# One pair of tiles in 97 fetched row by row from the sync queue, with a ring of 16 slots and frees that lag eight pairs

## The chip, the cores and the metric

The kernel runs on one core of a Trainium2 chip. The metric is the device time of one execution in microseconds (us), as the median of several; "ns" is nanoseconds. The engines are TensorE (PE; its weight loads are shown as PEld), VectorE (DVE), ScalarE (ACT), GpSimd (POOL) and SyncE (SP). Each has its own instruction queue with its own sequencer, which also executes the register arithmetic and the branches of that engine's loops. In rows of the trace a "q" behind the engine (PEldq, SPq) marks such an instruction.

## The reference, cut to what matters

It is one layer of a graph network with 6250 nodes of 256 values and 100,000 edges `src, dst`, ordered by `dst`:

```python
xn = layernorm(x)
h = norm * (xn @ W.T + bias)              # norm = rsqrt(1 + degree of the node)
agg = segment_sum(h[dst], src)            # 100,000 gathered rows, summed by src
x = x + norm * (agg + h) + linear_attention(xn) * gate @ Wproj + bproj
x = x + ffn(layernorm(x))                 # for the nodes with the best scores alone
```

The feed-forward part is computed for every node and added only to the nodes with the highest scores (KEEP = 6250 / 2 - 1 of them). The part that matters here is `h[dst]` summed by `src`: 100,000 rows of a table in HBM have to be fetched and added into 6250 sums.

## The kernel before

The work falls into four stages. First (to about 235 us) normalisation, degree histogram and gate, while VectorE sorts the edges by the window of their `src` node (a window is 125 nodes, there are 50). Then (to about 340 us) TensorE and ScalarE compute `h` and store it as `table` in HBM, 6250 rows of 512 float16 values (the high and the low part of 256 values), 1 KB each; this overlaps with attention sums until about 381 us. The third stage is the long one, to about 1339 us. The last is the selection and the store of the output.

In the long stage the 100,000 edges stand in 782 tiles of 128, taken in pairs: 391 pairs ("blocks" in the code, `NBLK`). Four queues work on them in step:

- **GpSimd** (lines 425 to 435) issues one indirect DMA for each tile: 128 row numbers from a column of `col_of`, 128 rows of `table` into one slot of `gath`. Ahead of a pair it waits for the semaphore `freed`.
- **SyncE** (lines 374 to 383) waits for the landing of each pair in order and adds 1 to `arrived`. Then, for the first 34 pairs at each and later at every fourth, it loads from `due_row` how many visits TensorE must have made to be done with the pair `LAG` = 3 back, waits for `visits` to reach that, and raises `freed`. The ring is `ROUND` = 17 pairs of slots.
- **VectorE** builds, for each visit, two 128x128 one-hot matrices (line 1271) in a ring of `HOTS` = 8 visits.
- **TensorE** adds the pair into the window's sums in bank 0 with two 128x512 matmuls (line 812). A pair that lies on the border of two windows is visited in both: 458 visits. The loop is a real one (`counted`, lines 303 to 313): each turn has a few instructions of the sequencer. Line 309 holds five register operations in one fused instruction (the copy of the counter, the counter plus 1, `made`, `q % ROUND`, `made % HOTS`), line 812 twice a fused instruction of six multiplications and additions that make the two addresses, and line 312 the branch.

Around the visits of window `w` TensorE does the feed-forward of the window before and the attention and projection of the next (`window`, lines 872 to 885), and the projection needs what VectorE makes from the sums just finished (`summed`, `normed`, `gated`). Before its visits each window loads three numbers (lines 796 to 798) and adds its own rows (line 802).

Of the kernel before, what the change touches and what calls it, by code (L numbers as in the profile page):

```python
# [10 lines left out]
I32 = mybir.dt.int32  # L11
# [4 lines left out]
NODES, C, EDGES = 6250, 256, 100000  # L16
# [16 lines left out]
NB = 34  # L33
GROUP = 2
GEDGE = GROUP * TILE
ROUND = NB // GROUP
HOTS = 8
NOH = HOTS * GROUP
NBLK = (EDGES + GEDGE - 1) // GEDGE
NROUND = NBLK // ROUND  # L40
assert NROUND * ROUND == NBLK
PAD_ROW = NODES + 3 * NW - 1
LAG = 3
NXR = 4
DUE_MAX = 32000
LEVELS_IN_GROUP = 5
# [19 lines left out]
SEARCH = sum(STEPS)  # L66
FREED_BY = 4
FREED_ALONE = 2 * ROUND
NB_KT = 2
PEEK_FROM, PEEK, PEEK_LEAD = 10, 12, -26  # L70
PEEK_DEALT, KMAX_AFTER = 10, 16
# [19 lines left out]
def gps_layer(nc, x, src, dst, W, bias, Wqkv, Wproj, bproj, ln_g, ln_b, Wg1, bg1, Wg2, bg2,  # L91
              wr, br, w1, b1, w2, b2, out):
    table = nc.dram_tensor("table", (NODES, PART), F16, kind="Internal").ap()
    ctx = ExitStack()
    with ctx:
        def sb(name, shape, dt=F32):
            return ctx.enter_context(nc.sbuf_tensor(name, shape, dt))

        def sem(name):
            return ctx.enter_context(nc.semaphore(name))  # L100
# [13 lines left out]
        col_of = sb("col_of", [128, COLS], I32)  # L114
        row_of = sb("row_of", [128, COLS])
        e_int = keyB[0:EP, 0:EC].bitcast(I32)
        gath = sb("gath", [128, NB, PART], F16)
# [81 lines left out]
        gate_tmp = sb("gate_tmp", [128, NBLK])  # L199
        hg = gate_tmp[0:P, 2 * P:2 * P + 2 * GH].rearrange("p (j n) -> p j n", j=2)  # L200
        due_row = gate_tmp[0:1, :].bitcast(I32)
        table_of = sb("table_of", [P, 1])
        hgT = gate_tmp[0:GH + 1, 0:2 * P].rearrange("p (j n) -> p j n", j=2)
        kmax = sb("kmax", [128, 2])
# [13 lines left out]
        def part_of(n):  # L218
# [10 lines left out]
        xb = W_in[0:P, 0, :]  # L229
# [28 lines left out]
        names = ("edges wload wdown wmain const const2 wtp wev hotr hist stats normd rowsh wss wsc diag nwt bn bna bg1 kps cntp chain "  # L258
                 "counted tabs final issued outs xn tp hid main hgv gtp ghT gps gate hev split xstore "
                 "moved kT kmaxd cntd kmt kmx kmr kv ekv xnr ctxp sumcp sumtp sumtc vdone ctxn wqcp wqcd pads ranked dealt oh arrived visits freed due duerow selfused "  # L260
                 "op og pp xb xm sum xh low x1 st nt zed ge zwt ztp zT hp gelu yp yv base halves csum").split()
        s = {n: sem("s_" + n) for n in names}
        s_block = [sem(f"s_block{k}") for k in range(ROUND)]
        s_xr = [sem(f"s_xr{j}") for j in range(NXR)]
        s_hself = [sem(f"s_hself{j}") for j in range(2)]
        s_xt = [sem(f"s_xt{j}") for j in range(2)]
# [48 lines left out]
        @block.sync  # L315
        def _(sp):
            halves = ((0, SPRAY), (SPRAY, P))
            for lo, hi in ((0, SPRAY), (SPRAY, EP)):
                sp.dma_start(e_int[lo:hi, 0:EW], src_v[lo:hi, :]).then_inc(s["edges"], 16)
            for lo, hi in ((0, SPRAY), (SPRAY, EP)):  # L320
                sp.dma_start(col_of[lo:hi, 0:EW], dst_v[lo:hi, :]).then_inc(s["edges"], 16)
            sp.wait_ge(s["pads"], 2)
            for to, of in ((e_int, src_s), (col_of, dst_s)):
                sp.dma_start(to[0:EP:EP // (GROUPS * SPARE), EW:EW + 1], of).then_inc(s["edges"], 16)
            for q in range(NXL):
                for lo, hi in halves:
                    sp.dma_start(big_g[lo:hi, q * XCH:(q + 1) * XCH, :],
                                 x_v[lo:hi, q * XCH:(q + 1) * XCH, :]).then_inc(s_x[q], 16)
            late = [
                (proj[:, :, :], Wproj.rearrange("(c p) n -> p c n", p=128)),  # L330
                (bproj_bc[:, :], bproj.rearrange("(a n) -> a n", a=1).to_broadcast([P, C])),
                (b2_bc[:, :], b2.rearrange("(a n) -> a n", a=1).to_broadcast([P, C])),
                (wr_bc[:, :], wr.rearrange("n a -> a n").to_broadcast([P, C])),
                (br_bc[:, :], br.rearrange("(a n) -> a n", a=1).to_broadcast([P, 1])),
            ]
            for to, of in late:
                sp.dma_start(to, of).then_inc(s["wload"], 16)
            with nc.allow_non_contiguous_dma(reason="a short vector onto partitions"):
                sp.dma_start(b1_sb[:, :], b1.rearrange("(c p) -> p c", p=128)).then_inc(s["wload"], 16)

            sp.wait_ge(s["hist"], NHIST + 1)
            sp.wait_ge(s["xstore"], HELD)
            for n in range(HELD // 8):
                sp.dma_start(big_t[:, n * 8:(n + 1) * 8, 0:2 * P],
                             held[n][:, 0:8 * 2 * P].rearrange("p (w c) -> p w c", w=8)).then_inc(s["moved"], 16)
            sp.wait_ge(s["moved"], 16 * (HELD // 8))
            sp.wait_ge(s["kT"], HELD // 2)
            sp.dma_start(w1_sb[:, :, :], w1.rearrange("(c p) n -> p c n", p=128)).then_inc(s["wload"], 16)

            sp.wait_ge(s["ranked"], 1)  # L350
            for c, lo, hi in hands:
                to = (lo + c * LANES) % EP
                sp.dma_start(dealt_keys[to:to + hi - lo, c * HAND:(c + 1) * HAND],
                             ranked_keys[lo:hi, c * HAND:(c + 1) * HAND]).then_inc(s["dealt"], 16)

            def table_rows(m):
                n = m % NPARTS
                sp.wait_ge(s["split"], m + 1)
                for lo, hi in row_parts:
                    sp.dma_start(tab_v[lo:hi, m, :], part_of(n)[lo:hi, :, :].rearrange("p a c -> p (a c)")).then_inc(s_tab[n], 16)  # L360

            for m in range(NW):
                table_rows(m)

            sp.wait_ge(s["tabs"], 1)
            sp.sem_inc(s["freed"], ROUND)

            sp.wait_ge(s["due"], 1)
            sp.wait_ge(s["gate"], NW)
            sp.dma_start(due_row[0:1, :].rearrange("a (i k) -> a i k", k=ROUND), visits_due[0:NROUND, :]).then_inc(s["duerow"], 16)  # L370
            sp.wait_ge(s["xnr"], NW)
            sp.dma_start(w2_sb[:, :, :], w2.rearrange("(c p) n -> p c n", p=128)).then_inc(s["wdown"], 16)
            sp.wait_ge(s["duerow"], 16)
            freed = ROUND
            for q in range(NBLK):
                sp.wait_ge(s_block[q % ROUND], 16 * GROUP * (q // ROUND + 1))
                sp.sem_inc(s["arrived"], 1)  # L377
                free = ROUND + q + 1 - LAG
                if freed < free and freed < NBLK and (q < FREED_ALONE or q % FREED_BY == 0):
                    due = sp.value_load(due_row[0:1, q:q + 1], min_val=1, max_val=DUE_MAX)  # L380
                    sp.wait_ge(s["visits"], due)
                    sp.sem_inc(s["freed"], free - freed)
                    freed = free
            for lo, hi in out_groups:
                sp.wait_ge(s["final"], hi)
                sp.dma_start(out_v[0:SPRAY, lo:hi, :], big_g[0:SPRAY, lo:hi, :]).then_inc(s["outs"], 16)
            sp.wait_ge(s["outs"], 2 * 16 * len(out_groups))

        @block.gpsimd
        def _(g):  # L390
# [31 lines left out]
            for n in range(NPARTS):  # L422
                g.wait_ge(s_tab[n], tab_landed(NW, n))
            g.wait_ge(s["tabs"], 1)
            for q in range(NBLK):
                if q * GROUP == FIRST_LANES * LANES:
                    g.wait_ge(s["tabs"], 2)
                if q == ROUND - 6 // GROUP:
                    g.wait_ge(s["vdone"], 1)
                g.wait_ge(s["freed"], q + 1)  # L430
                for tile in range(q * GROUP, (q + 1) * GROUP):
                    g.indirect_dma_start(  # L432
                        out=gath[:, tile % NB, :], out_offset=None, in_=table[:, :],
                        in_offset=bass.IndirectOffsetOnAxis(ap=col_of[:, tile:tile + 1],
                                                            axis=0)).then_inc(s_block[q % ROUND], 16)

        @block.scalar
        def _(a):
# [190 lines left out]
        def _(t):  # L629
# [164 lines left out]
            def sums(w, j, nth):  # L794
# [9 lines left out]

                with counted(t, f"sums{next(loops)}", first, end) as (q, upto):
                    made = q + before
                    for value in (made, q % ROUND, made % HOTS):
                        t.compute_val(value)
                    t.wait_ge(s["arrived"], upto)
                    slots, hot_slots = bass.ds(q % ROUND, 1), bass.ds(made % HOTS, 1)  # L810
                    for u in range(GROUP):
                        last = t.matmul(bank[0][:, 0:PART],  # L812
                                        onehot_g[:, hot_slots, u * 128:(u + 1) * 128].rearrange("p a r -> p (a r)"),
                                        gath_g[:, slots, u * PART:(u + 1) * PART].rearrange("p a c -> p (a c)"),
                                        start=False, stop=False, skip_group_check=True)
                        if u == 0:
                            last.wait_op(s["oh"], t.lower_val(made), "sem-ge")
                    last.then_inc(s["visits"], 1)
# [676 lines left out]
```

## Time and profile before

| what | value |
|---|---|
| median of 3 runs | 1404.43 us (1404.09 to 1404.56) |
| the profiled execution | 1399.99 us, span 1398.3 us |
| PE / DVE / POOL / ACT busy | 80% / 71% / 57% / 27% |
| mean granted TensorE clock | 0.931 |
| gathers on GpSimd | 782, busy 753.5 us, idle ahead of them 267.6 us |

Busy shares are means over stages that are bound by different things, so the long stage has to be read by itself. Idle time of an engine costs nothing unless something waits for that engine at that moment. Register, branch and semaphore instructions aren't counted as busy, so a loop that is paced by its sequencer shows as an engine with small gaps released by "issue".

### The profile page before, as it was taken

What the parts mean: (1) busy time and instruction counts of PE and PEld (TensorE: products, weight loads), DVE (VectorE), ACT (ScalarE), POOL (GpSimd) and SP (SyncE); (2) the same over time, 40 slices, a digit from 0 to 9 for tenths busy, and PEclk for the clock granted to TensorE, in tenths of its full rate; (3) what the DMA queues carried; (4) which work ended last, traced back from release to release, by engine and by line L of the source; (5) the groups of instructions that cost most, each with busy time, mean ns of one, the idle gap of its engine ahead of it and who ended that gap; (6) DMA issues with size and microseconds to landing.
All of it is one profiled execution on the core that took longest, in us unless ns stands there. A gap on an engine that the chain in (4) does not pass through costs nothing.

```text
span 1398.3 us, 27721 instructions
## 1 busy us (share of the span) xinstructions
PE 1115.0 (80%) x6477; PEld 812.5 (58%) x6478; DVE 994.5 (71%) x3592; ACT 373.3 (27%) x1168; POOL 802.9 (57%) x851
## 2 busy tenths in 40 slices
PE   0488998999977888888888888878887888778853
PEld 0488887888644555555555566546555555445532
DVE  8999999999546666666666665666665666566667
ACT  5844466665411111111111111111111111111100
POOL 0000002542777777777777777777777777777710
PEclk9789999999979999999999999999999999999976
DMA  9000211333633444333443443444434443444305
GB/s 240 20 2 2 90 43 45 108 100 92 184 113 112 117 120 120 114 115 118 119 119 117 119 119 110 119 117 119 118 111 119 120 119 112 117 117 119 112 27 183
DMA packets 76391, 149.81 MB, mean 107 GB/s; under 512 B 17984, under 2 KB 48416, under 8 KB 75708
## 3 DMA queue, kind: packets, MB, share of 16 engines
q0 software_dynamic: 37536, 102.55, 25.4%
q1 hardware_dynamic: 17190, 25.56, 6.3%
q10 hardware_dynamic: 21606, 21.05, 5.1%
q8 instruction: 21, 0.34, 0.1%
q14 instruction: 38, 0.30, 0.1%
HBM read 132.83 MB, written 12.80 MB: 104 GB/s over the span
## 4 chain that ended last, share of the span: by engine, by line
PE 28%; POOL 23%; issue 14%; DVE 11%; DMA 3%; DVEq 2%; ACT 1%; SPq 0%; POOLq 0%; ACTq 0%
POOL gath L432 23%; PE bank L812 9%; PE bank L868 3%; PE bank L857 3%; PE bank L742 3%; PE bank L750 3%; PE bank L734 3%; DMA gath<-table,col_of 3%; DVE onehot L1271 3%; DVE big_g L1470 1%; DVE rs L1325 1%; PE bank L835 1%; PE bank L827 1%; DVE rs L1327 1%; DVEq L1271 1%
## 5 line engine op out<-in xcount | busy, mean ns | idle before, releaser
L432 POOL DMA_INDIRECT gath<-table,col_of x782 | 753.5, 964 | 267.6 <-issue 225.7
L812 PE MATMUL bank<-gath,onehot 128*128 x916 | 297.2, 426 | 109.5 <-SPq L377 55.2
L1271 DVE TENSOR_SCALAR onehot<-iota_b,row_of,minus_row 128x128 bf16 x916 | 253.5, 328 | 108.2 <-issue 72.2
L812 PEld LDWEIGHTS bank<-gath,onehot 128*128 x916 | 89.0, 97 | 315.4 <-DVE onehot L1271 145.8
L857 PE MATMUL bank<-vv,w_sb 128*128 128x125 f32 x1600 | 203.3, 288 | 0.9 <-ACT vv L598 0.9
L612 ACT ACTIVATE WT<-bank,norm 125x256 f32<-125x256 f32 x50 | 23.7, 473 | 657.7 <-PE bank L819 657.7
L857 PEld LDWEIGHTS bank<-vv,w_sb 128*128 128x128 f32 x1600 | 196.8, 204 | 1.8 <-ACT vv L598 1.7
L868 PE MATMUL bank<-w_sb,keyB 128*125 128x256 f32 x800 | 184.6, 384 | 0.0
L1301 DVE SCALAR_TENSOR_TENSOR WT<-bank,norm,WT 125x256 f32<-125x256 f32 x50 | 24.2, 484 | 197.8 <-ACT WT L612 192.3
L868 PEld LDWEIGHTS bank<-w_sb,keyB 128*125 128x125 f32 x800 | 147.6, 190 | 20.0
L604 ACT ACTIVATE keyB<-bank,b_sb 128x125 f32<-128x125 f32 x400 | 113.0, 366 | 163.2 <-PE bank L857 163.2
L420 POOL TENSOR_TENSOR parts<-h_s,parts 125x256 f16<-125x256 f32 x30 | 26.2, 878 | 204.3 <-ACT parts L541 204.0
L639 PE MATMUL bank<-gath,big_t 128*128 128x50 bf16 x800 | 40.4, 230 | 39.6 <-DVE big_t L986 39.6
L802 PE MATMUL bank<-parts,ident_b 125*128 125x512 f16 x50 | 19.7, 395 | 59.1 <-issue 59.0
L639 PEld LDWEIGHTS bank<-gath,big_t 128*128 128x128 bf16 x800 | 39.8, 121 | 40.3 <-DVE big_t L986 40.3
L986 DVE TENSOR_SCALAR big_t<-onehot 128x200 bf16<-128x200 bf16 x500 | 61.4, 219 | 0.1
L827 PE MATMUL bank<-big_t,Wqc 128*128 (+1 forms) x400 | 60.6, 301 | 0.0
L835 PE MATMUL bank<-proj,W_in 128*125 128x256 f32 x200 | 52.7, 386 | 5.5 <-DVE W_in L1283 5.5
L827 PEld LDWEIGHTS bank<-big_t,Wqc 128*128 128x128 f32 x400 | 55.4, 214 | 0.1
L734 PE MATMUL bank<-WT,big_t 128*125 128x256 f32 x200 | 51.0, 383 | 1.9 <-ACT Wqc L541 1.2
L750 PE MATMUL bank<-vv,xn 125*128 125x257 f32 x200 | 51.7, 380 | 0.6 <-ACT xn L552 0.6
L742 PE MATMUL bank<-gath,big_t 128*125 128x256 f32 x200 | 51.4, 379 | 0.0
(296 smaller groups left out, 1541.8 us busy)
## 6 DMA issues: line engine op xcount, KB each, us to landing
gath<-table,col_of POOLq DMA_INDIRECT x782, 2.8
w_sb<-in_x ACTq DMA_DIRECT2D x50, 125.0 KB
parts<-table ACTq DMA_DIRECT2D x50, 125.0 KB
h_s<-in_x ACTq DMA_DIRECT2D x50, 125.0 KB
big_g<-in_x SPq DMA_DIRECT2D x5, 1120.0 KB
out<-big_g SPq DMA_DIRECT2D x8, 560.0 KB
table<-parts SPq DMA_DIRECT2D x30, 112.0 KB
table<-Wqc SPq DMA_DIRECT2D x20, 112.0 KB
```

The costliest lines, as they stand in the source:

```text
L432: g.indirect_dma_start(out=gath[:, tile % NB, :], out_offset=None, in_=table[:, :], in_offset=bass.IndirectOffsetOnAxis(ap=col_of[:, tile: ...
L604: a.activation(hid[:, k, :], bank[5 + k // 4][:, (k % 4) * P:(k % 4 + 1) * P], ACT.Gelu_apprx_tanh, bias=b1_sb[:, k:k + 1]).then_inc(s["ge ...
L639: last = t.matmul(bank[3][:, 0:NW], hot_row[:, u // RUN, :, u % RUN], hot_win[:, u // RUN, :, u % RUN], start=False, stop=False, skip_grou ...
L734: t.matmul(bank[j][0:P, 0:C], xnT[:, m, c, :], WT[:, c, :], start=c == 0, stop=False)
L742: t.matmul(bank[4 + j][0:P, 0:C], xnT[:, m, c, :], qkv[:, c, C:2 * C], start=c == 0, stop=False)
L750: last = t.matmul(bank[6 + half][:, 0:C + 1], ek[:, j, half * 128:(half + 1) * 128], x_n[:, j, 0:C + 1], start=m == 0, stop=m == NW - 1, s ...
L812: last = t.matmul(bank[0][:, 0:PART], onehot_g[:, hot_slots, u * 128:(u + 1) * 128].rearrange("p a r -> p (a r)"), gath_g[:, slots, u * PA ...
L827: last = t.matmul(bank[1][:, half * P:(half + 1) * P], Wqc[:, c, half * 128:(half + 1) * 128], xnT[:, bass.ds(m, 1), c, :].rearrange("p a ...
L835: last = t.matmul(bank[3][0:P, 0:C], ogT[:, c, :], proj[:, c, :], start=c == 0, stop=c == 1)
L857: last = t.matmul(bank[5 + k // 4][:, (k % 4) * P:(k % 4 + 1) * P], w1_sb[:, c, k * 128:(k + 1) * 128], zT[:, c, :], start=c == 0, stop=c ...
L868: last = t.matmul(bank[7][0:P, 0:C], hid[:, k, :], w2_sb[:, k, :], start=k == 0, stop=k == HC - 1)
L1271: last = nc.vector.tensor_scalar(onehot_g[:, slots, u * 128:(u + 1) * 128].rearrange("p a r -> p (a r)"), iota_b[:, :], row_of[:, bass.ds( ...
```

## The change

`LAG` is 8. The ring is `RING` = 16 pairs (slots 0 to 31 of the 34), and slots 32 and 33 belong to four pairs, q = 96, 193, 290 and 387 (every 97th). These are not gathered by GpSimd, which so issues 774 indirect DMAs. SyncE fetches them: four small DMAs first turn their 256 row numbers each into one row of `own_rows` (in `Wg2_b`, idle by then). Then, spread over some 90 turns of its loop, it loads eight row numbers at a time into registers and issues a 1 KB DMA for each row, 1024 in all. TensorE's loop computes the slot of a pair by a longer expression. The core of the diff:

```diff
-LAG = 3
+LAG = 8
+RING = ROUND - 1
+PERIOD = 97
+NOWN = NBLK // PERIOD
+NPOOL = NBLK - NOWN
+OWN_FROM = 5
+OWN_UNTIL = PERIOD - 3
+AT_ONCE = 8
...
-            sp.sem_inc(s["freed"], ROUND)
+            sp.sem_inc(s["freed"], RING)
...
+            sp.wait_ge(s["tabs"], 2)
+                for k in range(NOWN):
+                    q = k * PERIOD + PERIOD - 1
+                    sp.dma_start(own_rows[k:k + 1, :].rearrange("a (p u) -> a p u", u=GROUP),
+                                 col_of[:, q * GROUP:(q + 1) * GROUP]).then_inc(s["turned"], 16)
...
+            def gather_own(k, upto):
+                for n in range(given, upto):
+                    if n % AT_ONCE == 0:
+                        sp.load(rows, own_rows[k:k + 1, n:n + AT_ONCE])
+                    row = sp.snap(rows[n % AT_ONCE], min_val=0, max_val=NODES - 1)
+                    sp.dma_start(gath[n // GROUP:n // GROUP + 1, RING * GROUP + n % GROUP, :],
+                                 table[bass.ds(row, 1), :]).then_inc(s["own"], 16)
...
+                k, at = divmod(q, PERIOD)
+                i = q - k
+                if at == PERIOD - 1:
+                    sp.wait_ge(s["own"], 16 * GEDGE * (k + 1))
+                else:
+                    sp.wait_ge(s_block[i % RING], 16 * GROUP * (i // RING + 1))
                 sp.sem_inc(s["arrived"], 1)
-                free = ROUND + q + 1 - LAG
+                passed = q + 1 - LAG
+                free = RING + passed - passed // PERIOD
...
+                if k < NOWN:
+                    first = LAG if k == 0 else OWN_FROM
+                    if at == first:
+                        given = 0
+                        if k == 0:
+                            sp.wait_ge(s["vdone"], 1)
+                            sp.wait_ge(s["turned"], 16 * NOWN)
+                        else:
+                            sp.wait_ge(s["visits"], due_at(k * PERIOD - 1 + LAG))
+                            sp.sem_inc(s["ownfree"], 1)
+                    if first <= at <= OWN_UNTIL:
+                        upto = GEDGE * (at + 1 - first) // (OWN_UNTIL + 1 - first)
+                        gather_own(k, upto)
...
-            for q in range(NBLK):
+            for i in range(NPOOL):
+                q = i + i // (PERIOD - 1)
...
                     made = q + before
-                    for value in (made, q % ROUND, made % HOTS):
+                    slot = RING - (RING - (q - q // PERIOD) % RING) * (1 - q % PERIOD // (PERIOD - 1))
+                    for value in (made, slot, made % HOTS):
                         t.compute_val(value)
                     t.wait_ge(s["arrived"], upto)
-                    slots, hot_slots = bass.ds(q % ROUND, 1), bass.ds(made % HOTS, 1)
+                    slots, hot_slots = bass.ds(slot, 1), bass.ds(made % HOTS, 1)
```

## Rows read from the trace of the kernel before

**Rows 1.** The page: the costliest groups (busy, mean | idle before, releaser).
```profile
L432 POOL DMA_INDIRECT gath<-table,col_of x782 | 753.5, 964 | 267.6 <-issue 225.7
L812 PE MATMUL bank<-gath,onehot 128*128 x916 | 297.2, 426 | 109.5 <-SPq L377 55.2
```

**Rows 2.** One line's instructions (duration ns min/median/max, first and last start): L432.
```profile
L432 POOL DMA_INDIRECT gath<-table,col_of x782: 940/946/2256, 341.1 to 1335.0; - x196
```

**Rows 3.** Waits of GpSimd: us in total, times, longest.
```profile
POOL gath L432 <- issue: 225.7, 741, 0.3
...
POOL gath L432 <- SPq L382: 14.3, 39, 2.7
```

**Rows 4.** Waits of TensorE, 381 to 816 us.
```profile
PE bank L812 <- SPq L377: 7.2, 33, 0.2
```

**Rows 5.** Waits of TensorE, 816 to 1338.9 us.
```profile
PE bank L812 <- SPq L377: 48.0, 67, 2.3
```

**Rows 6.** Timeline of TensorE in window 23: start, length, idle before.
```profile
816.04 0.39 PE L802 MATMUL bank<-parts,ident_b 125*128 125x512 f16 x1 [1.67 <-issue]
816.57 0.60 PE L812 MATMUL bank<-gath,onehot 128*128 x2
...
824.71 0.60 PE L812 MATMUL bank<-gath,onehot 128*128 x2 [1.75 <-SPq L377]
```

**Rows 7.** Timeline of TensorE in window 2.
```profile
426.20 0.58 PE L802 MATMUL bank<-parts,ident_b 125*128 125x512 f16 x1 [1.48 <-issue]
...
430.94 0.60 PE L812 MATMUL bank<-gath,onehot 128*128 x2 [0.20 <-issue]
431.80 0.60 PE L812 MATMUL bank<-gath,onehot 128*128 x2 [0.25 <-SPq L377]
432.60 0.60 PE L812 MATMUL bank<-gath,onehot 128*128 x2 [0.20 <-SPq L377]
433.40 0.60 PE L812 MATMUL bank<-gath,onehot 128*128 x2 [0.20 <-SPq L377]
```

**Rows 8.** Instructions of L309, L812, L312 and L854, one line each.
```profile
L309 DVEq FUSED_REGOPS  x458: 197/199/244, 369.8 to 1332.1; - x153
L309 PEldq FUSED_REGOPS  x458: 179/183/212, 380.6 to 1335.8; - x153
...
L812 PEldq FUSED_REGOPS  x916: 74/74/89, 380.9 to 1338.4; - x184
...
L312 PEldq COMPARE_BRANCH  x458: 69/201/244, 381.3 to 1338.5; - x153
...
L854 PEldq FUSED_REGOPS  x48: 42/42/42, 411.4 to 1319.1; - x48
```

**Rows 9.** Timeline of all engines between two windows' visits.
```profile
565.94 0.17 PE L819 MATMUL bank<-zeros_b,ident_b 128*128 128x8 bf16 x1
...
573.63 0.42 DVE L1283 SCALAR_TENSOR_TENSOR W_in<-big_g,bank 128x250 f32<-128x250 f32 x1
...
574.29 1.03 PE L835 MATMUL bank<-proj,W_in 128*125 128x256 f32 x4
...
576.60 0.38 PE L802 MATMUL bank<-parts,ident_b 125*128 125x512 f16 x1 [1.29 <-issue]
```

**Rows 10.** Timeline of VectorE: the one-hots of that window.
```profile
574.18 0.54 DVE L1271 TENSOR_SCALAR onehot<-iota_b,row_of,minus_row 128x128 bf16 x2
...
581.20 0.54 DVE L1271 TENSOR_SCALAR onehot<-iota_b,row_of,minus_row 128x128 bf16 x2 [0.24 <-PE bank L812]
...
582.43 0.42 DVE L1293 TENSOR_TENSOR keyA<-bank,W_in 125x256 f32<-125x256 f32 x1
```

**Rows 11.** DMA issues and number loads on the sequencers of ScalarE and SyncE.
```profile
L557 ACTq DMA_DIRECT2D parts<-table x50: 265/270/291, 364.5 to 1303.9; - x50
...
L360 SPq DMA_DIRECT2D table<-Wqc x40: 316/402/880, 236.6 to 315.2; - x40
...
L380 SPq TENSOR_LOAD <-gate_tmp x117: 262/268/478, 375.3 to 1302.3; - x117
L380 SPq FUSED_REGOPS  x117: 147/147/192, 375.8 to 1302.6; - x117
```

**Rows 12.** SyncE's own waits.
```profile
SPq L382 <- PE bank L812: 371.9, 73, 20.6
```

More of the change, by code:

```diff
@@ L201, in gps_layer @@
         due_row = gate_tmp[0:1, :].bitcast(I32)
+        own_rows = Wg2_b[0:NOWN, :].bitcast(I32)
         table_of = sb("table_of", [P, 1])
@@ L260, in gps_layer @@
                  "moved kT kmaxd cntd kmt kmx kmr kv ekv xnr ctxp sumcp sumtp sumtc vdone ctxn wqcp wqcd pads ranked dealt oh arrived visits freed due duerow selfused "
-                 "op og pp xb xm sum xh low x1 st nt zed ge zwt ztp zT hp gelu yp yv base halves csum").split()
+                 "op og pp xb xm sum xh low x1 st nt zed ge zwt ztp zT hp gelu yp yv base halves csum own ownfree turned").split()
         s = {n: sem("s_" + n) for n in names}
-        s_block = [sem(f"s_block{k}") for k in range(ROUND)]
+        s_block = [sem(f"s_block{k}") for k in range(RING)]
         s_xr = [sem(f"s_xr{j}") for j in range(NXR)]
@@ L373, in _ @@
             sp.wait_ge(s["duerow"], 16)
-            freed = ROUND
-            for q in range(NBLK):
-                sp.wait_ge(s_block[q % ROUND], 16 * GROUP * (q // ROUND + 1))
+            sp.wait_ge(s["tabs"], 2)
+            with nc.allow_non_contiguous_dma(reason="row numbers of one block, two from each partition"):
+                for k in range(NOWN):
+                    q = k * PERIOD + PERIOD - 1
+                    sp.dma_start(own_rows[k:k + 1, :].rearrange("a (p u) -> a p u", u=GROUP),
+                                 col_of[:, q * GROUP:(q + 1) * GROUP]).then_inc(s["turned"], 16)
@@ new lines, in _ @@
+            rows = [sp.alloc_register(f"own_row{n}") for n in range(AT_ONCE)]
+            given = 0
[6 more added lines that the diff above has]
+                                 table[bass.ds(row, 1), :]).then_inc(s["own"], 16)
@@ L377, in _, with due_at @@
+            def due_at(q):
+                return sp.value_load(due_row[0:1, q:q + 1], min_val=1, max_val=DUE_MAX)
+            freed = RING
+            for q in range(NBLK):
+                k, at = divmod(q, PERIOD)
[4 more added lines that the diff above has]
+                    sp.wait_ge(s_block[i % RING], 16 * GROUP * (i // RING + 1))
                 sp.sem_inc(s["arrived"], 1)
-                free = ROUND + q + 1 - LAG
@@ L379, in _ @@
-                if freed < free and freed < NBLK and (q < FREED_ALONE or q % FREED_BY == 0):
-                    due = sp.value_load(due_row[0:1, q:q + 1], min_val=1, max_val=DUE_MAX)
-                    sp.wait_ge(s["visits"], due)
+                passed = q + 1 - LAG
+                free = RING + passed - passed // PERIOD
+                if freed < free and freed < NPOOL and (q < FREED_ALONE or q % FREED_BY == 0):
+                    sp.wait_ge(s["visits"], due_at(q))
                     sp.sem_inc(s["freed"], free - freed)
@@ L383, in _ @@
                     freed = free
+                if k < NOWN:
+                    first = LAG if k == 0 else OWN_FROM
+                    if at == first:
+                        given = 0
+                        if k == 0:
[7 more added lines that the diff above has]
+                        gather_own(k, upto)
+                        given = upto
@@ L424, in _ @@
             g.wait_ge(s["tabs"], 1)
-            for q in range(NBLK):
+            for i in range(NPOOL):
+                q = i + i // (PERIOD - 1)
                 if q * GROUP == FIRST_LANES * LANES:
                     g.wait_ge(s["tabs"], 2)
-                if q == ROUND - 6 // GROUP:
+                if i == ROUND - 6 // GROUP:
                     g.wait_ge(s["vdone"], 1)
-                g.wait_ge(s["freed"], q + 1)
-                for tile in range(q * GROUP, (q + 1) * GROUP):
+                g.wait_ge(s["freed"], i + 1)
+                for u in range(GROUP):
+                    tile = q * GROUP + u
                     g.indirect_dma_start(
-                        out=gath[:, tile % NB, :], out_offset=None, in_=table[:, :],
+                        out=gath[:, i % RING * GROUP + u, :], out_offset=None, in_=table[:, :],
                         in_offset=bass.IndirectOffsetOnAxis(ap=col_of[:, tile:tile + 1],
-                                                            axis=0)).then_inc(s_block[q % ROUND], 16)
+                                                            axis=0)).then_inc(s_block[i % RING], 16)
         @block.scalar
```

## The prediction

> **What bounds the kernel now.** I read the page's costliest groups first. The gathers of GpSimd stand on top: 782, busy 753.5 us, with 225.7 us of idle time that "issue" releases [rows 1]. They start at 341.1 and the last at 1335.0 us [rows 2], so one takes 993.9 / 781 = 1.27 us. GpSimd's waits say that hardly anything held it up: 741 gaps of at most 0.3 us are its own overhead, and of the 14.3 us ahead of which SyncE's release stands, 39 x 0.3 = 11.7 are that overhead too. One wait of 2.7 us is left [rows 3]. So GpSimd runs at its own pace from its start to the end of the long stage.
>
> The second view is TensorE's waits for `arrived` (SyncE's L377), in two stretches. Up to 816 us there are 33, none over 0.2 us [rows 4], which is the gap that stands between two visits anyway (0.20 or 0.25 us [rows 7]). In that half TensorE never waits for a row; it eats up the 16 pairs of lead with which GpSimd started. From 816 us on the waits are 48.0 us in 67 [rows 5], single ones of 1.75 us in a window [rows 6]. Less 67 x 0.22 of loop gap that is 33 us. This is all the slack that TensorE has: would every pair be there in time, its last visit would end 33 us earlier, at about 1306 instead of 1339 us. GpSimd is the bound, but TensorE stands 33 us behind it over 958 us, 3%.
>
> Third, what TensorE does in a visit. Visits in a row start 0.80 to 0.86 us apart, 0.82 in the mean, and two matmuls fill 0.60 of it [rows 7]. The one-hots come at 0.78 us ((581.20 - 574.18) / 9 [rows 10]) and with a start 3 us earlier, so VectorE doesn't pace it. The sequencer does: line 309 takes 183 ns, the two address instructions 74 each, the branch 201 [rows 8], together 532 ns of 820. The other 288 ns are the handing out of six instructions (these four and two weight loads), 48 ns each.
>
> By the Trainium skill ("TensorE: Matmul & The Clock Gate", section "Wait — 56ns, not 53.3ns?") a sequencer that decodes matmuls in software spends about 62 ns on each, which binds when the array's work is shorter. By that alone two matmuls would need 124 ns of the visit, as an estimate from that page, and a visit would be bound by its matmuls; the trace puts the weight on the register instructions and the branch instead, so a count of matmuls doesn't price this loop.
>
> **The change part by part.**
>
> *Eight gathers fewer.* GpSimd issues 774 instead of 782, 8 x 1.27 = 10.2 us less. This counts only while GpSimd is the bound. TensorE's slack falls from 33 to 23 us.
>
> *Ring of 16.* GpSimd can stand 16 instead of 17 pairs ahead. It wasn't stopped but once, for 2.7 us [rows 3]. Cost 0 to 2.5 us (one pair) if GpSimd stays the bound; nothing if TensorE is.
>
> *LAG 8.* SyncE now waits for visits 371.9 us in 73 waits [rows 12], because it holds at three pairs past TensorE. At eight it holds less and has time for its rows; what is freed is still what TensorE has used. With 16 slots and 8 of lag GpSimd may run 8 pairs past the landed one, less 3 by the grouping in fours, and needs 2. Cost and gain 0.
>
> *The rows on SyncE.* Up to 256 / 87 = 2.9 rows a pair. The nearest row is ScalarE's DMA with a register address, 270 ns; SyncE's own take 316 to 402 and at worst 880 [rows 11]. With the register operations for two addresses (147 ns for three [rows 11]) and about 50 ns at each of three instructions I put a row at 0.27 + 0.15 + 0.15 = 0.57 us, bounds 0.45 and 1.15. Then 1.7 us a pair (1.3 to 3.3), and 0.3 for eight numbers loaded at once (0.27 + 0.15 per eight rows, twice counted for safety), the pair's own wait and its share of the visit counts: 2.0 us, where a pair comes each 2.54 us. It fits, behind GpSimd's pace; `arrived` is raised ahead of the rows, so the next signal isn't late. Cost 0, with a case below if a row costs over 0.8 us. The four turning DMAs and the waits for `tabs` and `vdone` lie before pair 8 is needed: 0. The wait before the second, third and fourth own pairs is for a pair 6 back, up to one window's pause without visits, in which TensorE isn't waiting: 0.
>
> By the Trainium skill ("DMA: Bandwidth & Descriptors", section "Issuing engines are not separate DMA queues") the sequencer's time to start a DMA is usually small relative to the DMA itself. For 1 KB rows this doesn't fit the rows here, where starting one holds a sequencer 0.27 us and more [rows 11]; with the rule taken as it stands the SyncE case below would have no chance, and the sum stays.
>
> *The slot expression.* This is the costly part. `q % ROUND` was one operation. Now the loop of TensorE computes q // 97, a subtraction, % 16, a subtraction from 16, q % 97, // 96, 1 minus that, a product, and again 16 minus. That is three divisions or remainders more and five to eight simple operations. All stand in the same serial sequencer, before the matmuls that wait for their address. Prices:
> - a simple operation: six take 74 ns, two 42 [rows 8], so 8 ns each over a base of 26;
> - a remainder: line 309 has three simple ones and two remainders in 183 ns; less 26 + 24 that is 133, 66 each. VectorE's line 309, with one remainder, takes 199, so up to 125 for one;
> - no fused instruction of this kernel holds over six operations. 4 + 9 to 12 operations need three instead of one: two more, each 48 + 26 = 74 ns.
>
> Sum per visit: 3 x 66 + 8 x 8 + 2 x 74 = 198 + 64 + 148 = 0.41 us. From below: divisions at 8 ns, four simple operations and one more instruction, 24 + 32 + 74 = 0.13. From above: 3 x 125 + 12 x 8 + 3 x 74 = 0.69. I take 0.41, the value from TensorE's own rows. Nothing hides it: in the first half no visit waits for rows or one-hots, and between windows (565.94 to 576.60 us [rows 9]) TensorE follows VectorE's chain from finished sums to L1283, then the projection, and only then the next visits. That pause of 10.7 us stays and the visits get longer: 7.5 us for nine become 11.2. Behind the visits VectorE's own work (it is done at 582.9 while TensorE visits until 584.9) waits for nothing.
>
> **The sum.** TensorE at its own pace ends at 1306. 458 visits x 0.41 = 188 us bring this to 1494, 155 us after the 1339 of now. Slack of 33 us is used in this sum. GpSimd, done by 1325 if left alone, gets stopped by a full ring and its eight gathers gain nothing. The tail behind 1339 (59 us) stays. The profiled execution has 1399.99 us (1398.3 of span); it goes to 1555, and the median, 4.4 us above it, to 1559. The point of indifference: (33 - 10) / 458 = 0.05 us a visit, under the lower bound of 0.13.
>
> **The rivals.**
> - *GpSimd stays the bound, faster.* If the longer arithmetic cost less than 0.05 us a visit (hidden while the array works), the time falls by 10.2 less at most 2.5 for the ring: 1394 to 1397. For it: GpSimd's rows run without a stop, and 0.22 us of a visit the array idles. Against: that idle time shows the array waits for the sequencer, not the other way; one further instruction alone costs more than 0.05.
> - *The costs cancel, no change.* At 0.05 to 0.06 us a visit.
> - *SyncE becomes the bound, slower still.* With rows at 1.15 us, 2.9 of them and 0.5 of the rest make 3.8 us a pair while it fetches, 4 x 90 pairs, and 391 pairs take about 1400 us from 375: ends near 1770 plus the tail, about 1830. It decides from 2.85 us a pair (1113 us of TensorE's new stage by 391), which is a row at 0.85. For it: L360's longest, 880 ns. Against: the medians.
> - *Cheap divisions.* The mechanism of the forecast at its lower half, 0.13 to 0.25 us: 60 to 115 less 33, 1431 to 1486.
>
> **How the numbers follow.** Forecast (TensorE-bound, 0.25 to 0.69 us a visit) 0.76; cheap divisions 0.12; SyncE-bound 0.06; faster 0.04; no change 0.02. A change within 0.2% (2.8 us) can't be told from none here. Faster 0.04, same 0.02, slower 0.94. The predicted time is 1559. The range leaves out the two small cases on the fast side, the lowest of the cheap ones and SyncE's: 1468 (0.21 us: 96 - 33 = 63) to 1655 (0.62 us: 284 - 33 = 251).
>
> **What would show it.** Three fused instructions on TensorE where line 309 stands now; visits 1.2 us apart with 0.6 of idle time released by "issue"; windows of 22 us instead of 18.6 to 20; waits for L377 near zero throughout; GpSimd's gathers 774, with long waits on SyncE's release (about 150 us in all). It is wrong if visits stay 0.85 us apart, if TensorE waits for L377 in the second half, or if SyncE is never found waiting for anything.

## The result and the profile after

The changed kernel takes 1767.38 us (median of 4), the kernel before 1404.26 beside it: 25.8% slower, ratio 1.2582, interval 1.2564 to 1.2601. The forecast was 1559 with a range of 1468 to 1655. The direction held, the size didn't: +363 us instead of +155.

The page after: first busy time, then TensorE's granted clock in 40 slices, then the costliest groups that answer to [rows 1]. The core's mean granted clock is 0.760, from 0.931.

```profile
PE 1311.0 (74%) x6477; PEld 889.5 (50%) x6478; DVE 988.3 (56%) x3592; ACT 379.1 (21%) x1168; POOL 793.3 (45%) x843
...
PEclk9699999976676686776777777676777676776766
...
L482 POOL DMA_INDIRECT gath<-table,col_of x774 | 744.0, 961 | 614.3 <-SPq L416 369.3
L863 PE MATMUL bank<-gath,onehot 128*128 x916 | 429.0, 567 | 336.8 <-issue 143.6
```

The gathers number 774 as intended, but GpSimd now stands idle 369.3 us behind SyncE's release (L416, the former L382), where it had 14.3 [rows 3]. And SyncE, in the same profile, waits for visits of TensorE and hardly for rows: 10.6 us for landings (seven waits), 598.7 for visits. Its own waits, us in total, times, longest:

```profile
SPq L416 <- PE bank L863: 598.7, 56, 16.7
...
SPq L411 <- DMA gath<-table,col_of: 6.0, 4, 2.2
SPq L411 <- DMA gath<-table: 4.6, 3, 1.8
```

So TensorE is the bound. Its timeline within a window, the matmuls of four visits, against [rows 7]:

```profile
798.45 1.03 PE L863 MATMUL bank<-gath,onehot 128*128 x2 [0.62 <-issue]
800.11 1.03 PE L863 MATMUL bank<-gath,onehot 128*128 x2 [0.63 <-issue]
801.71 1.03 PE L863 MATMUL bank<-gath,onehot 128*128 x2 [0.58 <-issue]
803.37 1.03 PE L863 MATMUL bank<-gath,onehot 128*128 x2 [0.63 <-issue]
```

Visits stand 1.65 us apart instead of 0.82 (1.64 in the mean from 420 to 810 us), and behind each the array idles 0.6 us, waiting for nothing but its sequencer. The list of TensorE's waits puts 128.0 us of these gaps down to VectorE's one-hots and 65.2 to SyncE, because their semaphores came last by the profile. Neither held a visit up: the second one-hot of every visit ended at least 1.8 us ahead of its first matmul, and SyncE's gaps are as long as the others (0.64 us in the mean against 0.65). The instructions of the sequencer in a visit, against [rows 8] (line 317 was 309, 320 was 312, 863 was 812; 859 is new):

```profile
L317 PEldq FUSED_REGOPS  x458: 237/243/259, 381.8 to 1705.6; - x153
...
L859 PEldq MOVE  x1374: 29/29/38, 382.1 to 1706.4; - x197
L859 PEldq FUSED_REGOPS  x1374: 51/88/149, 382.2 to 1706.5; - x197
...
L863 PEldq FUSED_REGOPS  x916: 80/80/95, 382.9 to 1706.8; - x184
...
L320 PEldq COMPARE_BRANCH  x458: 82/223/245, 383.2 to 1707.0; - x153
```

1374 is 3 x 458: each visit has three moves and three fused instructions more, six where I had counted two. There are as many moves as constants on the left of a minus in the expression (16, 16 and 1). The reading is that such a constant isn't part of the operation but is moved into a register first, and that the move breaks the run of operations that would share one instruction; the version without such constants, below, has no moves. The sequencer is busy without a break: after each of the new instructions the next one starts 58 or 59 ns later in the median.

**Where the 363 us are.** TensorE's last visit ends 368 us later than before. The visits: 458 x (1.64 - 0.82) = 376, less the 33 of slack, 343. The two ends of a window's row of visits add to this: the first visit starts 1.25 us behind the start of the window's own rows (L852) instead of 0.52, and L870 starts 0.82 us behind the start of the last visit instead of 0.44. Together that is 1.11 us, of which one spacing (0.82) is already counted; 50 x 0.29 = 14.

The pause between L870, right behind a window's visits, and the next window's own rows has also grown. One of them, against [rows 9]:

```profile
777.58 0.21 PE L870 MATMUL bank<-zeros_b,ident_b 128*128 128x8 bf16 x1
...
785.40 0.42 DVE L1334 SCALAR_TENSOR_TENSOR W_in<-big_g,bank 128x250 f32<-128x250 f32 x1
...
788.91 0.39 PE L852 MATMUL bank<-parts,ident_b 125*128 125x512 f16 x1
```

That is 11.33 us where it was 10.66; over the last 47 pauses the mean is 11.19 against 10.85, +16 us. VectorE's part of it (to L1334) is as long as before, 7.7 us in both means. TensorE's feed-forward is longer: the projection (L886, the former L835) starts 10.04 us into the pause instead of 8.63. Most of this is taken back, as the own rows then follow 1.15 us behind the projection instead of 2.22. The windows table shows what came with it: in the same stretch the granted clock is 0.70 where it was 0.94. Columns: stretch, length, busy us of PE, PEld, DVE, ACT and POOL, then the clock. Before:

```profile
385.00:816.00 431.00, 355.86 (x1878) 237.66 (x1876) 278.67 (x1039) 66.65 (x221) 325.33 (x340) 0.94 0.40 117
```

After:

```profile
385.00:816.00 431.00, 318.43 (x1306) 194.32 (x1305) 194.22 (x731) 47.30 (x151) 237.90 (x250) 0.70 0.30 86
```

The first matmuls of the feed-forward, right behind the visits, before and after (after the bar stand busy us and the mean of one in ns, 301 and 413):

```profile
L827 PE MATMUL bank<-big_t,Wqc 128*128 (+1 forms) x400 | 60.6, 301 | 0.0
```

```profile
L878 PE MATMUL bank<-big_t,Wqc 128*128 (+1 forms) x400 | 94.1, 413 | 0.0
```

The two levels are 1.2 and 2.4 GHz, and 0.70 is a mix of them: most visits, with 0.6 us of idle array after each pair of matmuls, now run at the lower one (two matmuls 1.03 us instead of 0.60). In the window at 777.58 us the first 2.4 us of the pause are at the lower level still (0.50), and the stretch from 785.0 to 788.9 is at the full one (1.00). The visits don't suffer from it, as they have 0.6 us to spare; the pause does. That the idle gaps bring the level down wasn't tried by itself, and longer gaps didn't always come with a lower clock. In the experiments below the core's mean clock was 0.932 with gaps of 0.38 us, 0.946 with 0.32 to 0.36 and 0.862 with 0.56, where the kernel before has 0.931 with 0.22.

Two pauses are apart from the rest. Window 1's, 19.2 us before, is 11.5: before, TensorE waited there 3.0 us for VectorE's `lnb_wide` (L1341) at its start and 2.4 for `W_in` ahead of the projection, now for neither; -7.7. Window 0's is 2.3 longer, and the first visit of all starts 1.9 later. 343 + 14 + 16 - 7.7 + 2.3 + 1.9 = 370, against the 368 measured; 0.01 us in the spacing of the visits would be 4.6.

### The profile page after: what moved, and what is told of

Read it like the earlier page. It is cut to its first block, busy times and chain, and to the rows that moved or that the text cites. A ratio compares the mean times of both kernels' runs of the same rounds, so it can differ in the third digit from the quotient of the medians.

```text
span 1766.3 us, 33669 instructions
## 1 busy us (share of the span) xinstructions
PE 1311.0 (74%) x6477; PEld 889.5 (50%) x6478; DVE 988.3 (56%) x3592; ACT 379.1 (21%) x1168; POOL 793.3 (45%) x843
## 4 chain that ended last, share of the span: by engine, by line
DVE 26%; issue 19%; PE 19%; SPq 14%; DVEq 6%; ACT 1%; DMA 1%; ACTq 0%
PE bank L863 11%; DVE onehot L1322 9%; SPq L397 8%; SPq L395 3%; DVE rs L1376 2%; PE bank L792 2%; PE bank L784 2%; PE bank L800 2%; DVEq L1322 2%; DVE rs L1378 1%; DVEq L317 1%; DVE WT L1352 1%; SPq L396 1%; DVE rs L1377 1%; ACT WT L662 1%
## 5 line engine op out<-in xcount | busy, mean ns | idle before, releaser
L482 POOL DMA_INDIRECT gath<-table,col_of x774 | 744.0, 961 | 614.3 <-SPq L416 369.3
L863 PE MATMUL bank<-gath,onehot 128*128 x916 | 429.0, 567 | 336.8 <-issue 143.6
L863 PEld LDWEIGHTS bank<-gath,onehot 128*128 x916 | 93.5, 102 | 652.3 <-issue 436.0
L1322 DVE TENSOR_SCALAR onehot<-iota_b,row_of,minus_row 128x128 bf16 x916 | 247.4, 318 | 116.2 <-issue 96.8
L908 PEld LDWEIGHTS bank<-vv,w_sb 128*128 128x128 f32 x1600 | 224.8, 228 | 1.7 <-ACT vv L648 1.7
L908 PE MATMUL bank<-vv,w_sb 128*128 128x125 f32 x1600 | 224.7, 307 | 0.9 <-ACT vv L648 0.9
L878 PE MATMUL bank<-big_t,Wqc 128*128 (+1 forms) x400 | 94.1, 413 | 0.0
L878 PEld LDWEIGHTS bank<-big_t,Wqc 128*128 128x128 f32 x400 | 90.4, 330 | 0.2
L886 PE MATMUL bank<-proj,W_in 128*125 128x256 f32 x200 | 53.4, 391 | 3.1 <-DVE W_in L1334 3.1
L1088 DVE TENSOR_TENSOR keyB<-keyA 128x512 f32<-128x512 f32 (+2 forms) x74 | 49.5, 669 | 2.4
```

The source lines that it names most:

```text
L482: g.indirect_dma_start(out=gath[:, i % RING * GROUP + u, :], out_offset=None, in_=table[:, :], in_offset=bass.IndirectOffsetOnAxis(ap=col_ ...
L863: last = t.matmul(bank[0][:, 0:PART], onehot_g[:, hot_slots, u * 128:(u + 1) * 128].rearrange("p a r -> p (a r)"), gath_g[:, slots, u * PA ...
L878: last = t.matmul(bank[1][:, half * P:(half + 1) * P], Wqc[:, c, half * 128:(half + 1) * 128], xnT[:, bass.ds(m, 1), c, :].rearrange("p a ...
L908: last = t.matmul(bank[5 + k // 4][:, (k % 4) * P:(k % 4 + 1) * P], w1_sb[:, c, k * 128:(k + 1) * 128], zT[:, c, :], start=c == 0, stop=c ...
L1322: last = nc.vector.tensor_scalar(onehot_g[:, slots, u * 128:(u + 1) * 128].rearrange("p a r -> p (a r)"), iota_b[:, :], row_of[:, bass.ds( ...
```

## The experiments

Each was timed against the kernel before on the same chip, whose median there was 1401.9, 1404.2 and 1401.4 us in the three sets. Theory A is that TensorE's sequencer paces the long stage, so the price is the time of the register instructions in a visit; B that SyncE's rows cost the time. The other letters are those of the expectations. Comments behind a # in the diffs are mine.

**All pairs on GpSimd.** The changed kernel with SyncE's rows gone:

```diff
-            for i in range(NPOOL):
-                q = i + i // (PERIOD - 1)
+            for q in range(NBLK):
...
-                        out=gath[:, i % RING * GROUP + u, :],
+                        out=gath[:, (RING if own else i % RING) * GROUP + u, :],
...
-                        gather_own(k, upto)
```

> The changed kernel without SyncE's rows: GpSimd gathers all 391 pairs, the four own ones into the same slots 32 and 33; ring of 16, lag of 8 and TensorE's long slot expression stay. Theory A (TensorE's sequencer paces the long stage, 1.65 us a visit): the time stays at 1767, within 5, although 1024 DMAs are gone from SyncE and GpSimd has eight gathers more; visits 1.65 us apart. Theory B (SyncE's rows hold the signals or the DMA engines back): between 1404 and 1500. Theory C (both share the loss): between 1500 and 1750, and the difference to 1767 is the price of the rows.

1766.43 us, ratio 1.2600 (1.2575 to 1.2626), the same as with the rows (1.2582). The 1024 DMAs cost nothing that shows and the eight saved gathers give nothing; B and C fall. Visits 1.65 us apart here too.

**The same slots without a constant on the left.**

```diff
-slot = RING - (RING - (q - q // PERIOD) % RING) * (1 - q % PERIOD // (PERIOD - 1))
+slot = ((q - q // PERIOD) % RING + q % PERIOD // (PERIOD - 1) * RING).with_bounds(min_val=0, max_val=RING)
```

> The changed kernel with the same slot numbers written without a constant on the left of a minus: (q - q // 97) % 16 + q % 97 // 96 * 16. All four divisions and remainders stay, the three moves and two of the fused instructions go. Theory A with the price on the number of instructions: from rows of the changed kernel the first fused instruction grows from 243 to about 293 ns and one of about 150 with 58 of hand-out follows, so a visit takes about 1.16 us, 0.34 more than before: 458 x 0.34 = 156, less 33 of slack, 1527, and up to 28 more if the lower clock lengthens the pause between windows, 1555. Theory A with the price on the divisions: still near 1700. Theory B: unchanged at 1767.

1541.48 us (ratio 1.0994, 1.0976 to 1.1012), within what was expected: 225 us back by spelling alone. Visits stand 1.18 us apart in the mean, clock 0.862. The three moves and two of the three fused instructions are gone; this is all that line 859 has left:

```profile
L859 PEldq FUSED_REGOPS  x458: 162/169/169, 382.2 to 1479.4; - x153
```

All divisions and remainders are still there, and two simple operations fewer, so the larger part of the loss was the number of instructions.

**Ring of 16 and LAG 8 alone.**

```diff
-LAG = 3
+LAG = 8
...
-                        out=gath[:, tile % NB, :], out_offset=None, in_=table[:, :],
+                        out=gath[:, tile % (RING * GROUP), :], out_offset=None, in_=table[:, :],
```

> The kernel before with only a ring of 16 pairs and LAG 8: 782 gathers, no rows on SyncE, slot q % 16. Theory A: 1404, within 3 (GpSimd was never stopped by the ring but for 2.7 us; one pair less of lead costs TensorE's stage nothing). Rival D (the lead of 17 pairs or the tight lag carried something): slower by over 3.

1404.28 us against 1401.86 (ratio 1.0018, 1.0008 to 1.0027): 2.4 us slower, within what was expected, though not nothing. It is about one pair of GpSimd's work (2.54 us). That the shorter ring rather than the lag costs it wasn't separated.

**One division more.**

```diff
-                    for value in (made, q % ROUND, made % HOTS):
+                    slot = (q + q // 97 * ROUND) % ROUND
+                    for value in (made, slot, made % HOTS):
```

> The kernel before with one thing: the slot is (q + q // 97 * 17) % 17, the same number by one division, one product and one sum more, which also pushes made % 8 into an instruction of its own. Nothing else moves. Theory A: a visit grows by about 0.20 us (50 + 16 for the operations, 58 + 26 + 50 for the new instruction); 458 x 0.20 = 92, less the 33 of slack, +59: 1463, to 1490 with a lower clock. Theory B: 1404, there are no rows.

1448.75 us (ratio 1.0339, 1.0322 to 1.0356), +47, less than the 1463 to 1490 expected. Visits stand 0.99 us apart in the mean, 0.17 more: 458 x 0.17 = 78, less 33, +45. My price for the added operations and the new instruction was 0.03 us too high.

**One remainder more.**

```diff
+                    hot = made % 8000 % HOTS
-                    for value in (made, q % ROUND, made % HOTS):
+                    for value in (made, q % ROUND, hot):
```

> The kernel before with one remainder more in line 309's instruction (made % 8000 % 8, the same number), and nothing else. Theory A: a visit grows by about 50 ns, 458 x 0.05 = 23 us of TensorE, which is under its slack of 33: the time doesn't move (within 2 us), and TensorE's waits for rows in the second half fall from 48 to about 25. Rival E (every nanosecond in the visit counts, there is no slack): +23.

1405.89 us, +1.7 of the 18 us that the visits grew by in sum (ratio 1.0015, 1.0004 to 1.0026). It prices a remainder, line 309 against [rows 8]:

```profile
L309 PEldq FUSED_REGOPS  x458: 220/223/253, 383.4 to 1341.1; - x153
```

183 to 223: 40 ns for one remainder, not 66. Visits are 0.04 us longer, and TensorE's waits for rows from 816 us on fall from 48.0 to 25.8 us, as expected. The slack is there: E would have had about +18.

**The next window's numbers loaded ahead.**

```diff
                 if not last:
+                    look_up(w + 1)        # the three value_loads, into kept registers
                     project(w + 1)
```

> The kernel before, but TensorE loads the three numbers of the next window ahead of its projection instead of behind it, while VectorE's chain keeps it waiting anyway. Theory A: the pause between windows falls from 11.0 to about 9.8 us, TensorE catches up with GpSimd some ten windows earlier and waits for rows instead (about 100 us in all instead of 55), and the time stays within 2 us of before, since GpSimd is the bound. Rival E: 50 x 1.2 = 60 us less.

1402.38 against 1404.23 (ratio 0.9986, 0.9976 to 0.9995): 1.9 us of gain, 3.4 at the end of the interval. The pause shortened less than expected, to 10.57 us in the mean from 10.85, but the waits for rows are 91.7 us instead of 55.2:

```profile
PE bank L818 <- SPq L377: 91.7, 131, 2.3
```

The longer waits say that TensorE's extra speed turns into waiting, as GpSimd is the bound.

**The change with a cheap loop.** With what these had shown: own pairs where a remainder hits them, the counter read after its increment, so that exactly seven operations are left, which stand in one instruction, and the numbers ahead. VectorE's loop reads the counter the same way.

```diff
-PERIOD = 97
+PERIOD = 96
...
-                    slot = RING - (RING - (q - q // PERIOD) % RING) * (1 - q % PERIOD // (PERIOD - 1))
+                    slot = (q1 % RING + q1 % 96 // 95).with_bounds(min_val=0, max_val=RING)   # q1 = q + 1
...
-                        out=gath[:, i % RING * GROUP + u, :],
+                        out=gath[:, (q + 1) % RING * GROUP + u, :],
```

> The change made again with a cheap loop on TensorE: own pairs q = 94, 190, 286 and 382, slot = (q + 1) % 16 + (q + 1) % 96 // 95, read from the counter after its increment, so that all seven operations stand in one fused instruction; numbers of the next window loaded ahead; SyncE's rows, the ring of 16 and LAG 8 as in the change. Theory A: a visit takes about 0.92 us, TensorE keeps some 50 us of slack, GpSimd is the bound again with 774 gathers: 10.2 less than before, plus 2.5 for the shorter ring: 1394, between 1391 and 1397. Theory B (SyncE's 1024 rows cost more than they save): 1402 or above.

1396.99 us, ratio 0.9951 (0.9938 to 0.9965), and in a second set

> The same kernel as v1_every_96th, run beside its two controls on one chip: 0.5% below the kernel before (1397).

1394.22 us, ratio 0.9944 (0.9930 to 0.9958). It beats the kernel before by 7 us. The first is within the 1391 to 1397 expected. One instruction stands in line 317's place; its own row:

```profile
L317 PEldq FUSED_REGOPS  x458: 272/277/294, 381.3 to 1332.0; - x153
```

The timeline of TensorE shows visits 0.92 us apart (0.96 at others):

```profile
561.65 0.60 PE L867 MATMUL bank<-gath,onehot 128*128 x2 [0.36 <-issue]
562.57 0.60 PE L867 MATMUL bank<-gath,onehot 128*128 x2 [0.32 <-issue]
```

And among its waits it still waits for rows, so GpSimd is the bound:

```profile
PE bank L867 <- SPq L409: 64.7, 93, 2.0
```

**Its two controls.** First the same kernel, but GpSimd gathers the own pairs too:

> The version with own pairs every 96th and the cheap loop (v1_every_96th), but GpSimd gathers the four own pairs too (782 gathers, into the same slots) and SyncE fetches no rows. Theory A: GpSimd is the bound, eight gathers more are 10.2 us more: 1404 to 1407 where v1 had 1397. Rival F (v1's gain came from the cheap loop and the numbers loaded ahead, not from the gathers): 1397.

1400.79 us, ratio 1.0001 (0.9990 to 1.0012), faster than the 1404 to 1407 expected. Against the 1394.22 of `v1_again` in the same set it is 6.6 us: the gain is that of the eight gathers, of the 10.2 us expected from them, and why 3.6 are missing is open. The cheap loop with the numbers ahead does no more than pay for itself and the ring. F falls.

Then LAG 3 in place of 8:

```diff
-LAG = 8
+LAG = 3
```

> v1_every_96th with LAG 3 instead of 8. SyncE then holds at three pairs past TensorE, 372 us in the kernel before, and needs 1024 x 0.51 = 522 us of the 960 of the stage for rows. If the held time can't be used for rows, as the wait stands in the same queue, it has to catch up while TensorE visits: signals come late and the time is 1405 to 1440 (the lag is needed for the rows). Rival: the lag doesn't matter, 1397.

1414.08 us (ratio 1.0081, 1.0066 to 1.0097), 19.9 above `v1_again`. SyncE is held at visits and has the rows behind them in its queue:

```profile
SPq L414 <- PE bank L867: 235.3, 46, 10.2
```

In v1 these waits are 6.0 us in all. The lag isn't idle, then: it is what lets a queue that also signals do rows.

**Six own pairs.** v1 with every 64th pair:

> The same with six own pairs (every 64th): GpSimd issues 770 gathers, 12 fewer than before, and SyncE 1536 rows, 4.5 a pair. Theory A: 15.2 less, plus 2.5: 1389. SyncE needs 4.5 x 0.51 = 2.3 us of the 2.54 of a pair, with 0.3 for signals and visit counts behind it: if it falls behind, the signals for landed pairs come late, TensorE waits for them, and the time is 1395 to 1420.

1447.51 us, ratio 1.0298 (1.0284 to 1.0312), worse than the 1420 I gave as the worst. SyncE waits for landed pairs 51.2 us in all where v1's has 286.1, so it is the one that is late. Between 385 and 560 us, while it fetches the first own pair's 256 rows in 54 turns (4.7 a pair), GpSimd stands still behind it:

```profile
POOL gath L479 <- SPq L414: 49.6, 33, 6.5
```

What a row costs SyncE, of v1. The register operations of a row:

```profile
L395 SPq FUSED_REGOPS  x1024: 44/44/64, 385.1 to 1312.7; - x171
```

Its move and its DMA:

```profile
L396 SPq MOVE gath<-table x1024: 29/29/39, 385.2 to 1312.8; - x171
L396 SPq DMA_DIRECT2D gath<-table x1024: 217/218/313, 385.3 to 1312.9; - x171
```

And the load of eight numbers:

```profile
L394 SPq TENSOR_LOAD <-Wg_b x128: 524/780/963, 384.3 to 1307.6; - x128
```

Rows follow each other in 0.41 us, with an eighth of the load 0.51. Times 4.7 that is 2.4, and with 0.3 for signals and counts (the prediction's estimate) 2.7 a pair, over GpSimd's 2.54. The trace of the six-pair version has more: the first own pair's rows go out from 388.0 to 553.0 us, 3.05 us a pair, and the others take 149 to 150 us for 57 turns, 2.6 a pair. 54 x 0.51 and 5 x 57 x 0.08 make 27 and 23 us over GpSimd's pace, together the 50 us by which this version is slower than v1 in the same set. In the first stretch SyncE also loads a visit count at every pair up to the 34th, which may be the rest of its 3.05 us; that wasn't tried.

## Why the prediction was wrong

*The bound and the slack: right.* That TensorE stood 33 us behind GpSimd and would take its place at 0.05 to 0.07 us a visit is what the doses show: +0.17 us a visit gave +47 us, +0.04 gave 1.7.

*Eight gathers, ring, lag: right in kind.* The gathers gave nothing in the change and 7 us where TensorE had room. The ring and lag together cost 2.4 us, the upper end I had for one pair. That the lag gives SyncE time for its rows was right, but "cost and gain 0" doesn't price it: with rows and the cheap loop LAG 3 costs 20 us.

*The rows on SyncE: right,* 0.41 us a row against 0.57 forecast (0.51 with its share of the load, which the forecast counted apart), hidden behind the pace of the pairs. The SyncE case had its place right (it is what decides at 4.7 rows a pair) but not here. Its time of 1830 happens to lie nearer to the result than the forecast; the run without rows shows that it has no part in it. Its threshold was also off by the prediction's own terms: (2.85 - 0.5) / 2.9 is 0.81 us a row, not 0.85.

*The slot expression: the step that failed.* It was the right term and mis-sized, 0.41 us a visit where 0.82 was measured, and even my upper bound was 0.69. The price of a division was set too high (66 ns; a remainder measured 40). The number of instructions was set far too low: I counted operations and divided by six, which gave two more. There are six, three moves and three fused instructions, and respelling the three constants on the left of a minus took five of them away. Three moves at 29 ns, fused instructions of 129, 51 and 88 ns in the visit at 801 us, 60 on line 317 and 34 on the branch and the addresses make 449 ns; the other 370 or so are the handing out of six instructions, some 60 ns each, where I had 48.

*The clock: missing, but small.* I took the pause between windows as fixed. It grew by 0.34 us in a window, 16 us in all, at a granted clock of 0.70. At 1.18 us a visit (core's clock 0.862) it is 10.91 us and at 0.99 (0.932) 10.85, as before. The ends of a window's visits, 14 us, were missing too.

By the Trainium skill ("DMA: Bandwidth & Descriptors", section "Issuing engines are not separate DMA queues") the sequencer's time to start a DMA is usually small relative to the DMA itself. What a row's DMA takes by itself wasn't read here. Against the loop the starting isn't small: at 0.41 us for each KB it is what bounds the six-pair version.

## What to carry to other kernels

In a hardware loop whose engine idles between instructions that nothing but "issue" releases, count the sequencer's instructions, not operations: here each cost 50 to 60 ns to hand out before it did anything, and the spelling of one expression alone took the visit from 1.18 to 1.64 us. An offload from the bound engine is worth only the slack of the next one, so price what the offload adds to that one first. And a queue that has both to signal and to do slow work needs a lag long enough never to be held.

## What was not expected of the hardware

With the same slot numbers the kernel takes 1767 or 1541 us, by where a constant stands. A remainder takes 40 ns of a fused instruction, moving a constant 29 with some 60 for handing it out. In the stretch where pairs of matmuls stand 1.65 us apart the granted clock was 0.70 instead of 0.94, and it is the other work of the window that paid for it, 0.34 us each time. Loading eight numbers into registers takes SyncE 0.78 us where one takes 0.27 [rows 11].
